# Values of layer 0 weighed in five chunks of 128 head-and-key rows, brought to those rows through DRAM

## The chip, the cores and the metric

The kernel runs on one core of one Trainium2 chip. A core has TensorE (PE; PEld is its weight load), VectorE (DVE), ScalarE (ACT), GpSimd (POOL) and SyncE (SP, which here only issues DMAs and waits), and sixteen DMA engines. The metric is the device time of one execution in microseconds (us), the median of several runs; lower is better.

## The reference, cut to what matters

Two layers, each a cross attention and a mixture of eight experts with a residual path. The change is in the first attention: 32 sequences of 128 tokens (D = 128) look at 77 context rows each, with 8 heads of 64.

```python
q = (x @ Wq).reshape(B, N, 8, 64).transpose(0, 2, 1, 3)        # x: layernorm of the residual, 32 x 128 x 128
k = (context @ Wk).reshape(B, M, 8, 64).transpose(0, 2, 1, 3)  # context: 32 x 77 x 128
v = (context @ Wv).reshape(B, M, 8, 64).transpose(0, 2, 1, 3)
attn = softmax(einsum('bhnd,bhmd->bhnm', q, k) * scale)
out = einsum('bhnm,bhmd->bhnd', attn, v)
x = x + tanh(g_xattn[0]) * (out.transpose(0, 2, 1, 3).reshape(B, N, 512) @ Wo + bo)
# then: expert layer 0, attention of layer 1 (16 heads of 8), expert layer 1
```

## The kernel before

**Products of weights.** Both layer-0 products of two weight matrices are made once: `wqk` (Wq times Wk of a head) and `wvo` (Wv times Wo of a head, 128x128 for each head), each split in a high and a low part (fp32r). So for a sequence b the "value" of a head is directly its contribution to the output: `vo0[key, head, :]`, 77 keys by 8 heads by 128 floats.

**Units and steps.** A unit of layer 0 is one sequence. `attention0_steps` writes out by hand the order of the work: step u holds `score0(u)` (six matmuls into two PSUM banks), `exp0(u)`, `weigh0(u - 2)`, the two halves of the values `v0(u, 0)` and `v0(u, 1)` (four heads each, three matmul passes of 77x512 into the one bank `V_BANK`), `divide0(u)`, `turn0(u - 1)`, `bias0(u)`, and among them pieces of the keys of the next group of four sequences (`k0`), its layernorm (`norm`, `normalize`, `xt`), the routing tasks of groups that are already done (`mturn`, `route`, `pick`, `rank`, `lead`, `scatter`) and one background task a step (context blocks, `("tables", l)`, `("expert", 0, e)`). All five engines walk the same list in its order and each takes the tasks that concern it, so the list is the order of every engine's queue. SP runs ahead in it until something that it waits for isn't done.

**One unit of layer 0.** DVE takes the row maximum and subtracts it (L1243, L1246), ACT takes the exponential (L1122), DVE sums (L1297) and inverts, POOL divides (L1598). PE transposes the eight heads of 77 keys apart into two banks (`turn0`, L830), ACT copies both banks to `prob_t` (L1136; every fourth unit DVE copies the second one, L1305). ACT copies each half of the values from `V_BANK` to `vo0` (L1127), which PE must wait for before the next half. PE then adds up eight products of 77 rows (`weigh0`, L850); each is recorded as two instructions, sixteen in all. DVE adds the result to the residual (L1311).

```python
for head in range(NH0):
    done = pe.matmul(banks[:, O_BANK, 0:D], prob_t[0:NKEY, b % 2, head, :], vo0[:, b % 2, head, :],
                     start=head == 0, stop=head == NH0 - 1)
```

**Layer 1** already works in chunks: 8 heads of 77 keys lie one behind the other, 616 rows, cut into `CHUNKS` = 5 chunks of 128, 128, 128, 128 and 104 rows. `turn1` transposes five chunks (L840) and `weigh1` adds up five products (L866, ten recorded instructions).

**Waits.** `w.wait_ge(name, n)` blocks the engine until a semaphore has reached n; everything behind it on that engine waits too. A DMA adds 16 when it has landed.

Of the kernel before, what the change touches and what calls it, by code (L numbers as in the profile page):

```python
# [17 lines left out]
ALU = mybir.AluOpType  # L18
ACT = mybir.ActivationFunctionType
# [6 lines left out]
P = 128  # L26
# [251 lines left out]
def order():  # L278
# [3 lines left out]
    out += first[1:] + [("wvo", 0), ("wvo", 1), ("ctx", 1), ("gates",)]  # L282
# [24 lines left out]
def flamingo_two_layers(nc, a, out):  # L307
# [49 lines left out]
    y_rows = [nc.dram_tensor(f"y_rows{k}", [(2 * HT + NO_TOKEN) * P, D], F32, kind="Internal").ap() for k in range(2 * HALVES)]  # L357

# [4 lines left out]
    with ExitStack() as stack:  # L363
        def sbuf(name, shape, dt=F32):
            return stack.enter_context(nc.sbuf_tensor(name, shape, dt))
# [71 lines left out]
        prob_t = sbuf("prob_t", [P, 2, UH, SEQ])  # L437
# [63 lines left out]
        vo0 = layer0_only.enter_context(nc.sbuf_tensor("vo0", [NKEY, 2, NH0, D], F32))  # L501
# [101 lines left out]
        def _(sync):  # L603
# [29 lines left out]
            for t in plan:  # L633
# [25 lines left out]
                elif t[0] == "tail":  # L659
# [3 lines left out]
                    sync.dma_start(x_rows[k][bass.ds(r, P), :], empty_rows[e * P:(e + 1) * P, :]).then_inc(sem("tails"), 16)  # L663
                elif t[0] == "fetch":
# [73 lines left out]
        def _(pe):  # L738
# [86 lines left out]
            def turn0(b):  # L825
                w.wait_ge("divided", b + 1)
                for k in (0, 1):
                    w.wait_ge(f"prob_t{k}", b)
                    for i in range(4):
                        done = pe.transpose(banks[0:NKEY, PT_BANK[k], i * SEQ:(i + 1) * SEQ], prob[:, b % 2, 4 * k + i, :], ident[:, :])  # L830
                    done.then_inc(sem("prob_turned"))

            def turn1(u):
                flat = prob1_of(u).rearrange("p h n -> p (h n)")
                w.wait_ge("exp", NSEQ + u + 1)
                w.wait_ge("xb", LAYER_BLOCKS)
                for k, chunks in enumerate(CHUNK_SETS):
                    w.wait_ge(f"prob_t{k}", NSEQ + u)
# [4 lines left out]

            def weigh0(b):
                w.wait_ge("prob_t0", b + 1)
                w.wait_ge("prob_t1", b + 1)
                w.wait_ge("v0", 2 * b + 2)
                w.wait_ge("x_attn", b)
                for head in range(NH0):
                    done = pe.matmul(banks[:, O_BANK, 0:D], prob_t[0:NKEY, b % 2, head, :], vo0[:, b % 2, head, :],  # L850
                                     start=head == 0, stop=head == NH0 - 1)
                done.then_inc(sem("pv"))

            def weigh1(u):
                b, half = u // 2, u % 2
                width = UH * DV1
                w.wait_ge("prob_t0", NSEQ + u + 1)
                w.wait_ge("prob_t1", NSEQ + u + 1)
# [19 lines left out]
            for t in plan:  # L878
# [107 lines left out]
                elif kind == "turn":  # L986
# [3 lines left out]
                    for k in (0, 1):  # L990
                        w.wait_ge(f"prob_t{k}", NSEQ + layer * U1)
# [57 lines left out]
        def _(act):  # L1049
# [12 lines left out]
            for t in plan:  # L1062
# [60 lines left out]
                elif kind == "v0":  # L1123
                    b, h = t[1:]
                    w.wait_ge("v0_mm", 2 * b + h + 1)
                    w.wait_ge("pv", b - 1)
                    act.activation(vo0[:, b % 2, 4 * h:4 * h + 4, :].rearrange("p h d -> p (h d)"), banks[0:NKEY, V_BANK, :],  # L1127
                                   ACT.Copy).then_inc(sem("v0"))
                elif kind == "turn0":
                    b = t[1]  # L1130
                    for k in (0, 1):
                        if k == 0 or b % 4 > 0:
                            w.wait_ge("prob_turned", 2 * b + k + 1)
                            w.wait_ge("pv", b - 1)
                            dst = prob_t[0:NKEY, b % 2, 4 * k:4 * k + 4, :].rearrange("p s n -> p (s n)")
                            act.activation(dst, banks[0:NKEY, PT_BANK[k], :], ACT.Copy).then_inc(sem(f"prob_t{k}"))  # L1136
# [570 lines left out]
```

## Time and profile before

| | |
|---|---|
| three runs of the kernel before | 857.03, 858.85 and 860.1 us, median 858.85 |
| profiled execution | 851.79 us, of it 849.8 us from the first to the last instruction |
| busy: PE, PEld, DVE | 694.9 (82%), 630.4 (74%), 569.2 (67%) us |
| busy: ACT, POOL | 454.3 (53%), 478.6 (56%) us |
| mean granted TensorE clock | 0.95 of full |
| layer-0 attention | first `weigh0` at 45.0 us, last at 259.8 us |

The program is four phases one after the other, with small overlaps: layer-0 attention, its experts, layer-1 attention, its experts. Busy shares are means over all of them; what limits the first phase has to be read within it. A matmul record lasts longer than the distance to the next one, since matmuls are pipelined: how long a group of them holds PE is read from the chain of work, where each piece runs until the next begins.

### The profile page before, as it was taken

Reading aid. Unit: us, or ns where it says so; the run is one execution under the profiler, and the core shown is the slowest. Engines: PE = TensorE matmul, PEld = TensorE weight load, DVE = VectorE, ACT = ScalarE, POOL = GpSimd, SP = SyncE. Lnnn points to the kernel's source line nnn. Section 1 sums busy time; section 2 is a strip of 40 time slices with the busy share of each in tenths; the row PEclk is TensorE's granted clock in tenths of the full one; section 3 lists DMA queues with packets and bytes.
Section 4 is the critical chain, followed back from the end, with each engine's and each line's share of the span. In section 5 each row is a group of like instructions: output and inputs, shape, how many; then the busy total and the mean of one; then the engine's idle time right before and its main releaser. Section 6 shows DMA issues by size and latency. Waiting matters only on the chain.

```text
span 849.8 us, 17654 instructions
## 1 busy us (share of the span) xinstructions
PE 694.9 (82%) x5008; PEld 630.4 (74%) x5008; DVE 569.2 (67%) x2013; ACT 454.3 (53%) x1211; POOL 478.6 (56%) x693
## 2 busy tenths in 40 slices
PE   5899998997997668888879988988788847578688
PEld 4789987887886658777768887777678737567577
DVE  2668877886675555787887877977876725344553
ACT  3467675764555425555656776577476623233333
POOL 4233366664477555685554435667566766655562
PEclk9999999997999879999998999999999989799999
DMA  9334000001102222444633535533433022233445
GB/s 263 113 99 127 1 22 19 25 22 43 33 32 74 64 78 82 120 109 119 168 83 90 115 69 108 118 93 69 123 90 70 25 84 80 85 94 109 133 130 179
DMA packets 89934, 75.74 MB, mean 89 GB/s; under 512 B 28872, under 2 KB 78056, under 8 KB 89776
## 3 DMA queue, kind: packets, MB, share of 16 engines
q1 hardware_dynamic: 72144, 48.96, 23.3%
q0 software_dynamic: 9088, 19.68, 7.2%
q10 hardware_dynamic: 8608, 5.99, 2.5%
q8 instruction: 42, 0.69, 0.4%
q14 instruction: 52, 0.43, 0.2%
HBM read 44.99 MB, written 34.00 MB: 93 GB/s over the span
## 4 chain that ended last, share of the span: by engine, by line
PE 46%; DVE 20%; ACT 13%; issue 9%; another core or an unknown queue 8%; DMA 1%; DVEq 1%; POOL 0%; SPq 0%; POOLq 0%; ACTq 0%
PE banks L1003 8%; PE banks L1022 5%; PE banks L866 5%; PE banks L850 5%; PE banks L742 3%; DVE row_max L1243 3%; PE banks L806 2%; PE banks L744 2%; PE banks L925 2%; PE banks L743 2%; PE banks L830 2%; DVE prob L1246 2%; PE banks L840 2%; DVE hidden L1496 1%
## 5 line engine op out<-in xcount | busy, mean ns | idle before, releaser
L1677 POOL DMA_INDIRECT y_rows<-y_sb,result_at x156 | 152.8, 980 | 114.0 <-DVE result_at L1476 56.5
L1003 PE MATMUL banks<-xb,up 128*128 128x128 f32 x936 | 147.7, 298 | 65.0 <-ACT xb L1186 20.7
L1003 PEld LDWEIGHTS banks<-xb,up 128*128 128x128 f32 x936 | 128.1, 207 | 75.1 <-issue 43.1
L1670 POOL DMA_INDIRECT x_rows<-xm,row x128 | 127.5, 996 | 34.8 <-issue 30.4
L1022 PE MATMUL banks<-down,hidden 128*128 x624 | 104.6, 294 | 15.1 <-DVE y_sb L1513 6.7
L1022 PEld LDWEIGHTS banks<-down,hidden 128*128 128x128 f32 x624 | 89.0, 206 | 20.6 <-issue 20.2
L1632 POOL TENSOR_TENSOR v_flat<-v_raw,row_head 104x64 f32<-104x64 f32 (+1 forms) x128 | 55.9, 462 | 80.6 <-ACT v_raw L1165 80.0
L866 PE MATMUL banks<-v_flat,prob_t 128*128 128x108 f32 (+2 forms) x640 | 85.4, 282 | 6.7 <-ACT prob_t L1149 3.6
L866 PEld LDWEIGHTS banks<-v_flat,prob_t 128*128 128x128 f32 (+1 forms) x640 | 78.8, 195 | 16.0 <-ACT prob_t L1149 8.6
L1203 ACT ACTIVATE gate<-banks,block_bias 128x128 f32<-128x128 f32 x156 | 48.7, 365 | 74.9 <-PE banks L1003 47.8
L1243 DVE TENSOR_REDUCE row_max<-banks 128x8 f32<-128x616 f32 x96 | 75.8, 790 | 16.6 <-PE banks L821 8.9
L1598 POOL TENSOR_TENSOR prob<-prob,inv_sum 128x616 f32<-128x616 f32 x32 | 38.9, 1217 | 72.1 <-DVE inv_sum L1300 72.0
L1207 ACT ACTIVATE hidden<-banks 128x256 f32<-128x256 f32 x78 | 29.9, 384 | 92.3 <-remote 41.2
L1513 DVE COPY y_sb<-banks 128x128 f32<-128x128 f32 x78 | 22.4, 288 | 75.2 <-remote 35.9
L1496 DVE SCALAR_TENSOR_TENSOR hidden<-banks,block_bias,gate 128x128 f32<-128x128 f32 x156 | 47.0, 342 | 36.2 <-ACT gate L1203 29.8
L850 PE MATMUL banks<-vo,prob_t 77*128 77x128 f32 x512 | 64.7, 281 | 0.0
L850 PEld LDWEIGHTS banks<-vo,prob_t 77*128 77x128 f32 x512 | 63.0, 198 | 0.0
L1488 DVE COPY up<-up 128x256 f32 x156 | 56.1, 360 | 9.4 <-issue 3.9
L1149 ACT ACTIVATE prob_t<-banks 128x512 f32<-128x512 f32 (+1 forms) x128 | 48.8, 437 | 24.7 <-PE banks L840 24.6
L1246 DVE TENSOR_TENSOR prob<-banks,row_max 128x616 f32<-128x616 f32 x75 | 60.0, 800 | 2.6
L1165 ACT ACTIVATE v_raw<-banks 128x512 f32<-128x512 f32 x64 | 28.4, 444 | 44.8 <-PE banks L925 43.8
L1186 ACT ACTIVATE xb<-banks 128x128 f32<-128x128 f32 x156 | 43.4, 278 | 7.3 <-PE banks L993 3.3
(216 smaller groups left out, 1653.9 us busy)
## 6 DMA issues: line engine op xcount, KB each, us to landing
x_norm<-x_rows SPq DMA_DIRECT2D x86, 72.0 KB
x_far<-x_rows SPq DMA_DIRECT2D x70, 72.0 KB
gathered<-y_rows ACTq DMA_DIRECT2D x32, 128.0 KB
q_rows<-up_raw SPq DMA_DIRECT2D x8, 512.0 KB
q_even<-q_rows SPq DMA_DIRECT2D x12, 256.0 KB
q_odd<-q_rows SPq DMA_DIRECT2D x12, 256.0 KB
y_rows<-y_sb,result_at POOLq DMA_INDIRECT x156
k_rows<-up_raw SPq DMA_DIRECT2D x32, 77.0 KB
```

The lines of the kernel that those rows point to most:

```text
L850: done = pe.matmul(banks[:, O_BANK, 0:D], prob_t[0:NKEY, b % 2, head, :], vo0[:, b % 2, head, :], start=head == 0, stop=head == NH0 - 1)
L866: done = pe.matmul(banks[:, O_BANK, half * width:half * width + cols], prob_t[0:rows, u % 2, c, :], v1_flat[0:rows, first:first + cols], s ...
L1003: done = pe.matmul(banks[:, UP_BANK[i % 2], part * P:(part + 1) * P], block_w[:, i % WR, part // 2, part % 2 * P:(part % 2 + 1) * P], xb[: ...
L1022: done = pe.matmul(banks[:, Y_BANK[i % 2], 0:D], hidden[:, i % HR, half, :], of_expert(flat[:, (2 * layer + half) * D:], i, D), start=half ...
L1149: act.activation(dst, banks[0:rows, PT_BANK[k], 0:len(chunks) * SEQ], ACT.Copy).then_inc(sem(f"prob_t{k}"))
L1243: dve.tensor_reduce(m_view, s_view, AX.X, ALU.max).then_inc(sem("row_max"))
L1246: dve.tensor_tensor(prob_view.rearrange("p (k s) n -> p k s n", k=2), s_view, m_view.unsqueeze(3).to_broadcast([P, 2, 4, NKEY]), ALU.subtr ...
L1488: dve.tensor_copy(block_w[:, i % WR, 1 - layer, :], src[:, bass.ds(at, HID1)]).then_inc(sem("block_w_dve"))
L1496: dve.scalar_tensor_tensor(hidden[:, i % HR, half, :], banks[:, UP_BANK[i % 2], (2 + half) * P:(3 + half) * P], block_bias[:, k, 2 + half, ...
L1632: pool.tensor_tensor(v1_rows[0:rows, b % 2, half, chunks[0]:chunks[-1] + 1, :, 0:DK1], v1_raw[0:rows, chunks[0]:chunks[-1] + 1, half, :, : ...
L1670: pool.indirect_dma_start(out=x_rows[i // HG][:, :], out_offset=bass.IndirectOffsetOnAxis(ap=row[:, n, c:c + 1], axis=0), in_=xm[:, i % 2, ...
L1677: pool.indirect_dma_start(out=y_rows[k][:, :], out_offset=bass.IndirectOffsetOnAxis(ap=result_at[:, i % (2 * YR):i % (2 * YR) + 1], axis=0 ...
```

## The change

A unit's transposed probabilities and values are laid out as in layer 1: 616 rows of head and key in five chunks. The probabilities need no extra step, since `prob` lies in that order already. The values come out of the matmul with the key on the partition, so they go to DRAM and come back with head and key on it: each half of `vo0` (now one buffer a half) is written to `v_rows` by SP, and two loads fetch 4x128 and 104 rows into `vo_flat`. The values of sequence u + 1 are made in step u, a unit sooner than before, and those of sequence 0 ahead of step 0. ACT copies all of `prob_t` in layer 0; the two semaphores `prob_t0` and `prob_t1` become one. Two more semaphores (`group_sum`, `block_e`) are folded into `rank_step` and `table_step`, with the same waits.

```diff
         if u < NSEQ:
-            step += [("v0", u, 0), ("divide0", u)] + more[1]
+            step += [("v0_load", u)] + [("v0", u + 1, 0)][:u + 1 < NSEQ] + [("divide0", u)] + more[1]
         if 0 <= u - 1 < NSEQ:
             step.append(("turn0", u - 1))
         if u < NSEQ:
-            step += [("v0", u, 1), ("bias0", u)] + more[2]
+            step += [("v0", u + 1, 1)][:u + 1 < NSEQ] + [("bias0", u)] + more[2]
...
-    out += first[1:] + [("wvo", 0), ("wvo", 1), ("ctx", 1), ("gates",)]
+    out += first[1:] + [("wvo", 0), ("wvo", 1), ("ctx", 1), ("v0", 0, 0), ("v0", 0, 1), ("gates",)]
...
+    v_rows = [nc.dram_tensor(f"v_rows{i}", [UNIT_ROWS, D], F32, kind="Internal").ap() for i in (0, 1)]
...
-        prob_t = sbuf("prob_t", [P, 2, UH, SEQ])
+        prob_t = sbuf("prob_t", [P, 2, CHUNKS, SEQ])
...
-        vo0 = layer0_only.enter_context(nc.sbuf_tensor("vo0", [NKEY, 2, NH0, D], F32))
+        vo0 = layer0_only.enter_context(nc.sbuf_tensor("vo0", [NKEY, 2, NH0 // 2, D], F32))
+        vo_flat = layer0_only.enter_context(nc.sbuf_tensor("vo_flat", [P, 2, CHUNKS, D], F32))
...
+                elif t[0] == "v0":
+                    b, h = t[1:]
+                    half_rows = v_rows[b % 2][h * (UNIT_ROWS // 2):(h + 1) * (UNIT_ROWS // 2), :]
+                    w.wait_ge("v0", 2 * b + h + 1)
+                    w.wait_ge(f"v0_in{b % 2}", 32 * (b // 2))
+                    sync.dma_start(half_rows.rearrange("(a n) d -> n a d", n=NKEY), vo0[:, h, :, :]).then_inc(sem("v0_out"), 16)
+                elif t[0] == "v0_load":
+                    b = t[1]
+                    full = CHUNKS - 1
+                    w.wait_ge("v0_out", 32 * (b + 1))
+                    w.wait_ge("pv", b - 1)
+                    sync.dma_start(vo_flat[:, b % 2, 0:full, :], v_rows[b % 2][0:full * P, :].rearrange("(c p) d -> p c d", p=P)).then_inc(sem(f"v0_in{b % 2}"), 16)
+                    sync.dma_start(vo_flat[0:chunk_rows[full], b % 2, full, :], v_rows[b % 2][full * P:, :]).then_inc(sem(f"v0_in{b % 2}"), 16)
...
             def weigh0(b):
-                w.wait_ge("prob_t0", b + 1)
-                w.wait_ge("prob_t1", b + 1)
-                w.wait_ge("v0", 2 * b + 2)
+                w.wait_ge("prob_t", 2 * (b + 1))
+                w.wait_ge(f"v0_in{b % 2}", 32 * (b // 2 + 1))
                 w.wait_ge("x_attn", b)
-                for head in range(NH0):
-                    done = pe.matmul(banks[:, O_BANK, 0:D], prob_t[0:NKEY, b % 2, head, :], vo0[:, b % 2, head, :],
-                                     start=head == 0, stop=head == NH0 - 1)
+                for c, rows in enumerate(chunk_rows):
+                    done = pe.matmul(banks[:, O_BANK, 0:D], prob_t[0:rows, b % 2, c, :], vo_flat[0:rows, b % 2, c, :],
+                                     start=c == 0, stop=c == CHUNKS - 1)
                 done.then_inc(sem("pv"))
...
                 elif kind == "v0":
                     b, h = t[1:]
                     w.wait_ge("v0_mm", 2 * b + h + 1)
-                    w.wait_ge("pv", b - 1)
-                    act.activation(vo0[:, b % 2, 4 * h:4 * h + 4, :].rearrange("p h d -> p (h d)"), banks[0:NKEY, V_BANK, :],
+                    w.wait_ge("v0_out", 32 * b)
+                    act.activation(vo0[:, h, :, :].rearrange("p h d -> p (h d)"), banks[0:NKEY, V_BANK, :],
                                    ACT.Copy).then_inc(sem("v0"))
```

Left out: `turn0` now transposes the five chunks, as `turn1` does, through a helper `turn_chunks`; ACT's `turn0` copies 128x512 and 104x128; DVE's share of it is gone; the semaphore names.

Two places of the order. On TensorE, one step of the dense part before (`wvo_h` passes are `v0`, `wqk_h` passes are `k0`, `ident,prob` is `turn0`, `vo,prob_t` is `weigh0`):

```order
L850 MATMUL banks<-vo,prob_t 128x128 [waits x_attn,prob_t1,prob_t0]
L850 MATMUL banks<-vo,prob_t 128x128 x7
L742 MATMUL banks<-wvo_h,ctx_th 77x512 [waits v0]
L743 MATMUL banks<-wvo_h,ctx_tl 77x512
L744 MATMUL banks<-wvo_l,ctx_th 77x512
L742 MATMUL banks<-ctx_th,wqk_h 128x308 [waits split_lo]
L743 MATMUL banks<-ctx_th,wqk_l 128x308
L744 MATMUL banks<-ctx_tl,wqk_h 128x308
L830 MATMUL banks<-ident,prob 77x128 [waits divided]
L830 MATMUL banks<-ident,prob 77x128 x7
```

and the same place after the change (lines have moved by 14 to 17):

```order
L864 MATMUL banks<-vo_flat,prob_t 128x128 [waits x_attn,v0_in1,prob_t]
L864 MATMUL banks<-vo_flat,prob_t 128x128 x4
L759 MATMUL banks<-wvo_h,ctx_th 77x512 [waits v0]
L760 MATMUL banks<-wvo_h,ctx_tl 77x512
L761 MATMUL banks<-wvo_l,ctx_th 77x512
L759 MATMUL banks<-ctx_th,wqk_h 128x308 [waits split_lo]
L760 MATMUL banks<-ctx_th,wqk_l 128x308
L761 MATMUL banks<-ctx_tl,wqk_h 128x308
L846 MATMUL banks<-ident,prob 128x128 [waits divided]
L846 MATMUL banks<-ident,prob 128x128 x3
L846 MATMUL banks<-ident,prob 104x128
```

Eight products and eight transposes have become five and five; the half of the values between them now belongs to the next sequence.

On SP, the place of `("tables", 0)` and the first two experts after the change. Before, these loads stood alone there, with nothing of a unit between them, and SP issued the eight `up` loads one behind the other:

```order
L673 DMA v_rows<-vo 77x4x128 [waits v0_in1,v0]
L673 DMA v_rows<-vo 77x4x128 [waits v0]
L611 DMA down<-in_L_ffn_Wl_dram 128x8x128 [waits split_mm]
L611 DMA down<-in_L_ffn_Wl_dram 128x8x128
L611 DMA router<-in_L_ffn_Wr_dram 128x8x1
L611 DMA up_raw<-in_L_ffn_bl_dram 8x512
L611 DMA down_bias<-in_L_ffn_bl_dram 128x1024
L611 DMA router_b<-in_L_ffn_br_dram 128x8
L611 DMA select_b<-in_L_ffn_biases_N_dram 128x8
L679 DMA vo_flat<-v_rows 128x4x128 [waits pv,v0_out]
L680 DMA vo_flat<-v_rows 104x128
L673 DMA v_rows<-vo 77x4x128 [waits v0_in0,v0]
```

Four DMAs of a unit stand in SP's queue in every step now: two writes that wait for ACT, two loads that wait for the landing of both writes and for `weigh0` of two units before.

## Rows read from the trace of the kernel before

**Rows 1.** Windows: length, busy us and count of PE, PEld, DVE, ACT, POOL; PE clock, DMA share, GB/s

```profile
54.00:97.00 43.00, 43.00 (x319) 39.74 (x318) 33.49 (x87) 30.53 (x63) 17.28 (x26) 1.00 0.39 110
97.00:206.00 109.00, 97.71 (x708) 88.29 (x707) 86.38 (x304) 66.67 (x143) 66.50 (x89) 0.98 0.08 24
206.00:230.00 24.00, 21.99 (x129) 19.73 (x128) 13.50 (x50) 10.35 (x21) 10.14 (x14) 0.79 0.07 22
```

**Rows 2.** The chain of work, 54 to 262 us, shares by line

```profile
by line: PE banks L850 20.9%; PE banks L806 8.6%; PE banks L742 8.3%; PE banks L830 7.5%; PE banks L744 7.4%; PE banks L743 7.3%; issue 4.4%; ACT vo L1127 4.3%; DVE prob L1246 2.7%; PE banks L953 2.4%; DVE row_max L1243 2.4%; DVE m_stats L1
```

**Rows 3.** The chain in order of time (start, us, what), dense part

```profile
54.03 1.79 PE banks L850 x16
...
62.71 0.87 PE banks L830 x8
...
83.29 1.79 PE banks L850 x16
...
96.68 1.79 PE banks L850 x16
```

**Rows 4.** The chain in order of time, the part with routing

```profile
109.51 1.79 PE banks L850 x16
...
126.65 0.59 ACT vo L1127
...
133.58 0.58 ACT vo L1127
...
179.91 1.79 PE banks L850 x16
```

**Rows 5.** The chain in order of time, 205 to 240 us

```profile
205.75 3.42 PE banks L850 x16
...
218.40 2.31 PE banks L850 x16
...
231.52 1.79 PE banks L850 x16
...
236.89 1.79 PE banks L850 x16
```

**Rows 6.** Line 850: durations in ns (min/median/max), first and last start

```profile
L850 PE MATMUL banks<-vo,prob_t x512: 272/275/422, 45.2 to 259.8; 77*128 77x128 f32 x171
```

**Rows 7.** The chain in layer 1, where five chunks are weighed and transposed

```profile
463.15 1.34 PE banks L866 x10
...
464.92 0.55 PE banks L840 x5
```

**Rows 8.** ACT by shape in layer 1: busy us, mean ns, idle before

```profile
L1149 ACT ACTIVATE prob_t<-banks 104x128 f32<-104x128 f32 x64 | 17.8, 278 | 0.0
```

**Rows 9.** Timeline, the second half of the values of one unit (start, us)

```profile
134.21 0.45 PE L742 MATMUL banks<-wvo_h,ctx_th 128*77 128x512 f32 x1 [0.54 <-ACT vo L1127]
...
135.32 0.60 ACT L1127 ACTIVATE vo<-banks 77x512 f32<-77x512 f32 x1
```

**Rows 10.** Timeline, DMAs with a known end: last store; a write and its reader

```profile
847.67 0.34 ACTq L1232 DMA_DIRECT2D out_dram<-x_res  x1
...
412.40 0.45 SPq L688 DMA_DIRECT2D q_rows<-up_raw  x1
...
415.53 1.28 SPq L710 DMA_DIRECT2D q_even<-q_rows  x3
```

**Rows 11.** DMA view of 2 to 20 us, when the queues are full of 512-byte packets

```profile
DMA packets 10106, 5.20 MB, mean 289 GB/s; under 512 B 1104, under 2 KB 9722, under 8 KB 10106
```

**Rows 12.** Timeline of SP, the issues of the layer-0 tables

```profile
52.25 1.01 SPq L607 DMA_DIRECT2D down<-in_L_ffn_Wl_dram  x2
...
57.02 0.44 SPq L607 DMA_DIRECT2D select_b<-in_L_ffn_biases_N_dram  x1
```

**Rows 13.** Timeline, a pass of the values near the start of the phase

```profile
33.22 0.63 PE L742 MATMUL banks<-wvo_h,ctx_th 128*77 128x512 f32 x1
```

More of the change, by code:

```diff
@@ L823, in score1, with turn_chunks @@
                 done.then_inc(sem("scores"))
[L825 to L836, printed above, removed]
+            def turn_chunks(flat, n):
                 for k, chunks in enumerate(CHUNK_SETS):
-                    w.wait_ge(f"prob_t{k}", NSEQ + u)
+                    w.wait_ge("prob_t", 2 * n + k - 1)
                     for c in chunks:
@@ L856, in weigh1 @@
                 width = UH * DV1
-                w.wait_ge("prob_t0", NSEQ + u + 1)
-                w.wait_ge("prob_t1", NSEQ + u + 1)
+                w.wait_ge("prob_t", 2 * (NSEQ + u + 1))
                 w.wait_ge("v1", 4 * b + 4)
@@ L989, in _ @@
                     w.wait_ge(f"x_in{i % XR}", landed(i % XR, i + 1, XR))
-                    for k in (0, 1):
-                        w.wait_ge(f"prob_t{k}", NSEQ + layer * U1)
+                    w.wait_ge("prob_t", 2 * (NSEQ + layer * U1))
                     w.wait_ge("xb", i - 1)
@@ L1140, in _ @@
                     act.activation(prob1_of(u), prob1_of(u), ACT.Exp, scale=DK1 ** -0.5).then_inc(sem("exp"))
-                elif kind == "turn1":
-                    u = t[1]
+                elif kind in ("turn0", "turn1"):
+                    n = t[1] if kind == "turn0" else NSEQ + t[1]
+                    if kind == "turn1":
+                        w.wait_ge("up", LAYER_BLOCKS)
                     for k, chunks in enumerate(CHUNK_SETS):
                         rows = chunk_rows[chunks[0]]
-                        w.wait_ge("prob_turned", 2 * NSEQ + 2 * u + k + 1)
-                        w.wait_ge("pv", NSEQ + u - 1)
-                        w.wait_ge("up", LAYER_BLOCKS)
-                        dst = prob_t[0:rows, u % 2, chunks[0]:chunks[-1] + 1, :].rearrange("p s n -> p (s n)")
-                        act.activation(dst, banks[0:rows, PT_BANK[k], 0:len(chunks) * SEQ], ACT.Copy).then_inc(sem(f"prob_t{k}"))
+                        w.wait_ge("prob_turned", 2 * n + k + 1)
+                        w.wait_ge("pv", n - 1)
+                        dst = prob_t[0:rows, n % 2, chunks[0]:chunks[-1] + 1, :].rearrange("p s n -> p (s n)")
+                        act.activation(dst, banks[0:rows, PT_BANK[k], 0:len(chunks) * SEQ], ACT.Copy).then_inc(sem("prob_t"))
                 elif kind == "v1":
@@ L1300, in _ @@
                     dve.reciprocal(inv_sum[:, b % 2, 0:UH], row_sum[:, b % 2, :]).then_inc(sem("inv_sum"))
-                elif kind == "turn0" and t[1] % 4 == 0:
-                    b = t[1]
-                    w.wait_ge("prob_turned", 2 * b + 2)
-                    w.wait_ge("pv", b - 1)
-                    dve.tensor_copy(prob_t[0:NKEY, b % 2, 4:8, :].rearrange("p s n -> p (s n)"), banks[0:NKEY, PT_BANK[1], :]).then_inc(sem("prob_t1"))
                 elif kind == "weigh0":
@@ L1395, in _ @@
                     w.wait_ge("counts", i)
-                    dve.tensor_reduce(group_sum[:, :], picked[:, s, :, :].bitcast(F32).rearrange("p j e -> p e j"), AX.X, ALU.add).then_inc(sem("group_sum"))
-                    w.wait_ge("group_sum", i + 1)
+                    dve.tensor_reduce(group_sum[:, :], picked[:, s, :, :].bitcast(F32).rearrange("p j e -> p e j"), AX.X, ALU.add).then_inc(sem("rank_step"))
+                    w.wait_ge("rank_step", 3 * i + 1)
                     k = i // HG
```

33 lines of the change are left out of this document (16 added, 17 removed).

## The prediction

> **What bounds the kernel now.** I first cut the layer-0 attention, the only phase that the change touches, into stretches with the table of windows. From 54 to 97 us TensorE is busy for all of 43.0 us, DVE for 33.5 and ACT for 30.5; from 97 to 206 us, where routing is mixed in, TensorE has 97.7 of 109, DVE 86.4; from 206 to 230 us TensorE has 22.0 of 24 at a granted clock of 0.79 [rows 1]. Then I read the chain of work over 54 to 262 us: `weigh0` (L850) alone holds 20.9% of it and `turn0` (L830) 7.5%, and the six longest lines are all TensorE's [rows 2]. In order of time the chain shows what a piece costs where it counts: `weigh0` 1.79 us for its sixteen records, 0.112 us each, and `turn0` 0.87 us for eight, 0.109 each [rows 3]. Last, the chain of the routed part shows where TensorE isn't what ends last: after the `vo` copy at 126.65 us it goes through ACT and DVE (the routing's small operations, row maximum, subtraction) to ACT's exponential and the `vo` copy at 133.58 us behind it, for which TensorE stands still [rows 4]. A `weigh0` inside such a stretch is free today.
>
> **What is removed.** Six of sixteen records of `weigh0` go: 6 x 0.112 = 0.67 us a unit. Three of eight transposes go: 3 x 0.109 = 0.33 us. The nearest rows for the new shapes are layer 1's, which does the same five chunks: ten records 1.34 us, five transposes 0.55 us [rows 7]. The transposes agree (5 x 0.109 = 0.54); the ten records there are followed by a wait, so their 1.34 holds the tail of the last product, and 1.12 (10 x 0.112) is what I take where the next product follows at once; by 1.34 the saving would be 0.45. So 1.0 us a unit, at least 0.78. The units that profit are those whose pieces lie on the chain:
> - Dense, 54.03 to 96.68 us: seven units [rows 3], 7 x 1.0 = 7.0.
> - Routed, 97 to 206 us: the chain has nine `weigh0` (the first at 109.51, the last at 179.91 [rows 4]) and six `turn0`: 9 x 0.67 + 6 x 0.33 = 8.0.
> - 206 to 230 us: two slowed `weigh0` of 3.42 and 2.31 us [rows 5], of which 6/16 is 2.1, and a `turn0` slowed likewise: 2.7.
> - 230 to 248 us: two more units of 5.37 us (231.52 to 236.89 [rows 5]), 2.0.
> - The end, 248 to 262 us: two `weigh0` and a `turn0`, 1.7, and the last step has no values to make, so that the copy of the last probabilities comes that much sooner: 0.8. Together 2.5.
>
> That would be 22.2 us if nothing took its place.
>
> **What is added: a loop through DRAM.** ACT may overwrite `vo0` with a half of sequence b + 1 only once both halves of b have landed in DRAM (`v0_out`). So there is now a loop: copy of half 1 of b, its write, then ACT's copy of half 0 of b + 1, then TensorE's passes for half 1 (they need the one bank), then its copy. No row shows such a write, so I bound it. Low end: the last store starts its issue at 847.67 and the span ends at 849.8, 2.1 us for 64 KB of 128 packets [rows 10]. A half is 308 packets of 512 bytes; in full queues a packet takes 16 x 18 / 10106 = 0.0285 us of an engine [rows 11], so 180 packets more on 16 engines are 0.3 us: 2.4. High end: `q_rows`, 512 KB, has its issue at 412.40 and its reader's at 415.53, 3.1 us [rows 10]. I take 2.8, as a half in 512-byte pieces from 77 partitions is not tidier than either, and 0.1 for SP's wakeup: 2.9. The rest of the loop is two copies of 0.59 [rows 4], TensorE's three passes from start to copy, 1.1 (134.21 to 135.32 [rows 9]), and 0.05 for handing over: 2.3. A unit can't be shorter than 2.9 + 2.3 = 5.2 us.
> - Five dense units take 5.85 us now ((83.29 - 54.03) / 5), two 6.7 [rows 3]. The five would be 4.85 and stop at 5.2: 0.35 x 5 = 1.8 us not gained.
> - The units of 5.37 would be 4.4 and stop at 5.2 as well: 1.5 not gained.
> - Over the phase a unit is 6.9 us on the mean ((259.8 - 45.2) / 31 [rows 6]); in the routed part 5.2 never binds.
>
> So 22.2 - 3.3 = 18.9.
>
> The Trainium skill ("DMA: Bandwidth & Descriptors", "Why a DMA increments its semaphore by 16 and not by 1") says that a DMA from SP uses the largest number of engines up to 16 that divides the slowest dimension of both sides; for 77 partitions that is 11. It speaks against this write: 28 packets an engine instead of 19, 0.25 us more a landing, some 2.5 us less gained over the ten units that the loop binds. No row here shows how many engines a DMA took.
>
> **Loads.** Load b is issued once `weigh0(b - 2)` is done and the write has landed, and is needed two steps later, some 10 us. Its 616 packets are 616 x 0.0285 / 16 = 1.1 us [rows 11] on top of a landing like the above: hidden. Writes and loads together hold the DMA engines for 2.2 us of a unit; they are idle 92% of the routed part [rows 1].
>
> **Start.** The two halves of sequence 0 now stand ahead of `score0(0)`. TensorE's passes last 0.63 us there [rows 13], the three some 1.3; the second half must wait for the copy of the first (0.6), so scores begin 3.2 us later. TensorE has little slack behind, and ACT's first copy of step 0 waits for the first landing. Cost 3.0. From below it is 2.2, twice the 1.1 us from passes to copy of [rows 9].
>
> **SP's queue.** Its loads no longer run ahead. The layer-0 tables take SP from 52.25 to 57.46, 5.2 us [rows 12], and now stand between the write of one unit and the load and writes of the next: write (6, 1) leaves 5.2 + four issues of 0.45 [rows 10] = 7.0 us after (5, 1), where the loop has 5.2. That is 1.8 us, once; the second tables come in the routed part with its longer units: 0.2. Cost 2.0. The fetches of the first expert blocks now wait behind `v0_load(31)`, but the first is read two products and a transpose group later: nothing, and 1 us if that cover were gone. ACT's `prob_t` copies become 0.59 + 0.28 [rows 8] for two of 0.59, DVE loses eight copies: both leave slack. The folded semaphores wait for the same events: nothing.
>
> **Sum.** 18.9 - 3.0 - 2.0 = 13.9 us off the profiled 851.8: 837.9. That execution lies 7 us below the median of the runs shown, and nothing in the change touches that distance, so 858.85 - 13.9 = 845.
>
> **The rivals.**
> - **The landing is hidden** (chance 0.17). At 2.4 us the loop is 4.7 and binds almost nothing: 22.2 - 0.5, less 3.0 and 2.0, 16.7 off: 842. For it: SP has little else to do.
> - **DVE takes over** (0.15). In the routed part it has 86.4 us of 109 [rows 1]; with 8 us less it would be busy for 86%, in an order that makes it wait for others. If half the gain from 97 to 230 us goes into its waits, 8.5 are left: 850. Against it: its load falls a little, and its stretches are already counted as not gaining.
> - **The loop through DRAM sets every unit, and the kernel is slower** (0.09). It decides from the point where the loop is longer than the mean unit less what start and tables cost: 6.9 - 5/31 = 6.7 us, a landing of 4.4. At 5.0 the loop is 7.3, 31 x 0.4 + 5 = 18 us more: 877. For it: 512-byte packets, loads and expert weights in the same queue ahead of a write. Against: both ends of the bound are far below.
> - **Nothing to be seen** (0.05). TensorE has more gaps, and its clock falls: from 206 to 230 us it was 0.79 after a stretch with little work [rows 1]. Two more such stretches, each with 24 us of a fifth less clock, cost 10 us: 855 to 859. The Trainium skill ("TensorE: Matmul & The Clock Gate", "HAM oscillation") warns that gaps between bursts bring the half clock back; here the gap that I add is about 0.4 us a unit, and before, the 11 us that TensorE was idle in the routed part left it at 0.98.
>
> **How the numbers follow.** The forecast has 0.54. With the two rivals on its side, faster by over 0.3% (2.6 us, about what a measurement of this kernel can tell) has 0.86, no change 0.05, slower 0.09. The range: below, the hidden landing and a cheap start give 841, and up to 5 us more if routed stretches shrink beyond the chain's own pieces: 836. Above, DVE's 850, and 3 us for a landing at the high end and dear tables: 853. What lies outside is the slower rival, no change, and little else.
>
> **What would show it.** Right: `weigh0` ten records in 1.1 to 1.3 us on the chain; dense units of 5.2 us with ACT's first `vo` copy of a step released by a DMA; a later first `score0`; TensorE no longer full from 54 us on. Wrong: `vo` copies that wait over 1 us for a DMA in most units (landing over 3.5 us), a wait of `weigh0` for a load, or a routed part that still takes 109 us.

## The result, and the profile after

The changed kernel took 855.5 us (median of 17 runs, 850.54 to 861.21) where the kernel before took 859.5 (17 runs, 855.85 to 865.36). The ratio is 0.9950, 95% interval 0.9929 to 0.9971: 4 us faster, where 14 were forecast. The direction was right, the size was not, and 855.5 lies outside the range.

The sum was made on an execution of before that took 851.8 us, faster than every one of its 17 timed runs; the profiled execution of the changed kernel took 861.2. The stages must therefore be compared, not the two totals. These are windows of the changed kernel in the order of [rows 1], with one more at the end (length; busy us and count of PE, PEld, DVE, ACT, POOL; granted clock, DMA share, GB/s):

```profile
54.00:97.00 43.00, 38.72 (x251) 34.03 (x252) 32.47 (x80) 27.97 (x64) 17.33 (x26) 0.96 0.60 162
97.00:206.00 109.00, 93.13 (x589) 81.89 (x587) 88.45 (x303) 65.60 (x150) 66.74 (x88) 0.92 0.47 131
206.00:230.00 24.00, 19.02 (x104) 16.78 (x105) 15.22 (x58) 10.89 (x24) 11.71 (x17) 0.79 0.35 101
230.00:262.00 32.00, 27.00 (x160) 24.10 (x160) 19.69 (x66) 15.30 (x35) 22.09 (x30) 0.79 0.41 116
```

TensorE has less to do in the same 109 us (93.1 busy for 97.7), but at a granted clock of 0.92 for 0.98. Where the clock goes is seen in its timeline (start, us, work, in brackets the idle time before it and what ended it):

```profile
133.89 0.71 PE L846 MATMUL banks<-ident,prob 128*128 128x128 f32 x5
136.67 0.45 PE L759 MATMUL banks<-wvo_h,ctx_th 128*77 128x512 f32 x1 [2.07 <-ACT vo L1139]
...
138.60 1.37 PE L823 MATMUL banks<-k_t,xt_h 128*128 128x308 f32 x4
...
141.05 2.34 PE L864 MATMUL banks<-vo_flat,prob_t 128*128 128x128 f32 x10
```

After `turn0` TensorE stands still for 2.07 us, until ACT's copy of the first half of the values; in before this same gap was 0.54 us [rows 9]. From `score0` on what follows costs nearly double: its four records take 1.37 us and `weigh0` 2.34, where they take 0.8 and 1.3 in the same view at full clock. The windows behind two such gaps have a clock of 0.57:

```profile
110.00:114.00 4.00, 4.00 (x20) 3.95 (x19) 2.42 (x8) 2.90 (x8) 3.20 (x4) 0.57 0.54 144
137.00:143.00 6.00, 5.90 (x27) 5.45 (x26) 3.41 (x10) 3.85 (x9) 3.71 (x4) 0.57 0.41 115
```

ACT's copy is late because it stands behind the exponential, and that behind DVE. ACT's timeline in the gap:

```profile
135.42 0.72 ACT L1134 ACTIVATE prob<-prob 128x616 f32<-128x616 f32 x1 [3.13 <-DVE prob L1251]
136.04 0.57 ACT L1139 ACTIVATE vo<-banks 77x512 f32<-77x512 f32 x1
```

Over 54 to 262 us TensorE waits for that copy 17.8 us in 12 places (the view of waits: total, times, longest); below it the same view of the kernel before:

```profile
PE banks L759 <- ACT vo L1139: 17.8, 12, 2.9
```

```profile
PE banks L742 <- ACT vo L1127: 5.5, 6, 1.7
```

The other thing to see is a hold in SP's queue. The chain of work of the changed kernel, from 66 us on:

```profile
66.69 0.40 SPq L611
...
67.79 1.71 SPq L611
...
69.54 1.62 SPq L611
...
73.59 0.32 SPq L673
...
73.97 4.00 DMA v_rows<-vo
...
78.06 0.60 ACT vo L1139
...
81.67 1.93 PE banks L864 x10
```

The tables hold the queue from 66.69 us; the two loads of a unit follow at 72.59 and 73.02, and the two writes of the next unit's values at 73.59 and 73.97. The second one lands only at 78.0, with an expert's weights issued right behind it; ACT's copy waits for the landing, and `weigh0` then runs at a low clock again.

### The profile page after: what moved, and what is told of

It is laid out like the page before. It is cut to its first block, busy times and chain, and to the rows that moved or that the text cites. A ratio compares the mean times of both kernels' runs of the same rounds, so it can differ in the third digit from the quotient of the medians.

```text
span 859.4 us, 17242 instructions
## 1 busy us (share of the span) xinstructions
PE 684.9 (80%) x4720; PEld 618.0 (72%) x4720; DVE 566.5 (66%) x2005; ACT 448.8 (52%) x1219; POOL 480.2 (56%) x693
## 4 chain that ended last, share of the span: by engine, by line
PE 41%; DVE 23%; ACT 12%; issue 10%; another core or an unknown queue 7%; DMA 2%; SPq 1%; DVEq 1%; POOL 1%; ACTq 0%; POOLq 0%
PE banks L1015 10%; PE banks L1034 7%; PE banks L879 4%; DVE row_max L1248 4%; PE banks L864 3%; DVE prob L1251 3%; PE banks L759 2%; PE banks L846 2%; PE banks L823 2%; PE banks L938 2%; PE banks L761 2%; PE banks L760 2%; ACT x_norm L1117 2%; ACT vo L1139 1%
## 5 line engine op out<-in xcount | busy, mean ns | idle before, releaser
L1015 PE MATMUL banks<-xb,up 128*128 128x128 f32 x936 | 150.3, 302 | 66.4 <-ACT xb L1191 25.4
L1015 PEld LDWEIGHTS banks<-xb,up 128*128 128x128 f32 x936 | 130.8, 211 | 76.5 <-issue 41.4
L1034 PE MATMUL banks<-down,hidden 128*128 x624 | 104.9, 295 | 16.6 <-DVE y_sb L1513 10.4
L1154 ACT ACTIVATE prob_t<-banks 128x512 f32<-128x512 f32 x192 | 73.1, 436 | 24.7 <-PE banks L846 22.3
L1488 DVE COPY up<-up 128x256 f32 x156 | 53.6, 344 | 9.1 <-issue 4.2
L846 PE MATMUL banks<-ident,prob 128*128 128x128 f32 (+1 forms) x375 | 56.5, 284 | 0.0
L864 PE MATMUL banks<-vo_flat,prob_t 128*128 128x128 f32 (+1 forms) x320 | 48.1, 305 | 3.3 <-ACT prob_t L1154 3.3
L864 PEld LDWEIGHTS banks<-vo_flat,prob_t 128*128 128x128 f32 (+1 forms) x320 | 46.6, 222 | 3.4 <-ACT prob_t L1154 3.4
```

Source lines behind the costliest of these rows:

```text
L846: done = pe.transpose(banks[0:chunk_rows[c], PT_BANK[k], c % 4 * SEQ:(c % 4 + 1) * SEQ], flat[:, c * P:c * P + chunk_rows[c]], ident[:, :])
L864: done = pe.matmul(banks[:, O_BANK, 0:D], prob_t[0:rows, b % 2, c, :], vo_flat[0:rows, b % 2, c, :], start=c == 0, stop=c == CHUNKS - 1)
L1015: done = pe.matmul(banks[:, UP_BANK[i % 2], part * P:(part + 1) * P], block_w[:, i % WR, part // 2, part % 2 * P:(part % 2 + 1) * P], xb[: ...
L1034: done = pe.matmul(banks[:, Y_BANK[i % 2], 0:D], hidden[:, i % HR, half, :], of_expert(flat[:, (2 * layer + half) * D:], i, D), start=half ...
L1154: act.activation(dst, banks[0:rows, PT_BANK[k], 0:len(chunks) * SEQ], ACT.Copy).then_inc(sem("prob_t"))
L1488: dve.tensor_copy(block_w[:, i % WR, 1 - layer, :], src[:, bass.ds(at, HID1)]).then_inc(sem("block_w_dve"))
```

## The experiments

All kernels were compared with before on their own chip. There before took 792 us instead of 859. The 67 us do not lie in this phase: in a second profile of before `score0(25)` starts at 198.99 us, in the first at 199.13. So ratios are given, and 0.001 is 0.8 us. An interval of a ratio is 0.002 to 0.004 to each side.

What separates the kernels better is their profiles. This table has the start of `score0(n)` in us, read from TensorE's timeline of each, and the start of the last record of the last `weigh0`. Each row is one execution:

```
kernel       ratio    s(0)   s(1)   s(4)   s(8)  s(11)  s(25)  s(31) weigh0(31)
before       1       30.45  36.93  58.37  81.87 100.99 199.13 246.63 259.8
before_look  0.9998  30.44  36.81  58.24  81.73 100.84 198.99 248.59 261.8
after        0.9950  33.72  39.95  60.79  85.79 103.14 202.30 248.52 261.4
again        0.9948  33.74  39.98  61.62  86.98 103.84 201.12 246.66 259.4
pad          1.0018  33.84  40.07  61.35  86.56 105.65 207.15 250.90 264.1
nodma        0.9899  33.84  40.07  60.37  81.34  98.22 197.27 243.60 256.4
keep         0.9898  34.27  40.51  60.81  86.91 104.14 197.10 238.66 254.9
deep         0.9884  33.72  39.96  60.25  81.23  98.12 194.96 238.44 252.0
tables       0.9903  33.55  39.80  60.11  81.16  98.19 195.50 240.83 253.8
start        0.9964  29.79  39.47  60.99  86.74 103.38 201.76 247.13 260.7
best         0.9798  30.25  38.83  59.12  80.09  96.96 189.92 233.87 249.9
before_keep  1.0037  30.14  36.76  58.22  81.71 100.82 206.34 254.06 267.2
ideal        0.9834  30.14  36.52  56.80  77.78  94.66 187.65 229.28 246.3
best2        0.9872  34.15  40.38  60.67  81.64  98.52 191.51 232.98 249.0
keep_gaps    0.9911  34.20  40.43  60.73  86.16 103.20 196.42 238.01 250.7
best3        0.9830  30.16  39.10  59.41  80.39  97.25 190.26 231.65 245.2
best3_four   0.9808  29.68  38.30  59.30  80.28  97.14 190.41 236.75 249.5
ideal3       0.9815  30.17  36.54  56.85  77.85  94.71 187.75 229.22 241.8
```

The theories. **Clock**: the shorter work leaves longer gaps in the steps that DVE ends, in them TensorE's clock falls to half, and that gives the gain back. **Detour**: the way through DRAM and SP's queue costs it. **Order**: DVE ends last in the routed part, so that the gain turns into waits.

**again**, the changed kernel once more.

> The changed kernel once more, beside which the other kernels of this group stand. Both theories: 855 us, 0.995 of before. What it tells is how far the profiled execution of 861.2 us is from a usual one: if the half clock after the gaps of the routed part (109 to 114 us, 137 to 143 us) is there again, it belongs to the kernel; if the clock is at 1.00 there, that execution was an exception and the clock can't be what took the gain.

0.9948 (0.9922 to 0.9975), as in the first comparison; the clock in 97 to 206 us is 0.94, in 230 to 262 us 0.82, and in the two windows of 110 to 114 and 137 to 143 us 0.73 and 0.72. The half clock belongs to the kernel.

**before_look**, the kernel before once more.

> The kernel before once more, so that the profiled execution on which the prediction's sum was made can be set beside another one. If 851.8 us was an ordinary execution, its clock was 1.00 in 97 to 202 us and 230 to 262 us and will be so again, and score0(31) starts at 246.6 us; if it was a lucky one, the clock is lower in one of them and score0(31) comes 2 to 5 us later.

The same kernel to `score0(25)` within 0.2 us, then 2.0 us later at `score0(31)`: from 206 to 230 us its clock was 0.70, in the first profile 0.79 [rows 1]. Its row:

```profile
206.00:230.00 24.00, 23.26 (x124) 20.67 (x122) 12.39 (x48) 8.47 (x18) 9.94 (x13) 0.70 0.06 19
```

The first profile was 2 us lucky in this phase. Differences of 2 us behind 206 us are therefore not read as effects below.

**pad**, TensorE's records put back.

```diff
 def weigh0(b):
+    for c in (0, 1, 2):
+        pe.matmul(banks[:, O_BANK, 2 * D:3 * D], prob_t[:, b % 2, c, :], vo_flat[:, b % 2, c, :], start=True, stop=True)
...
 # turn_chunks, ahead of chunk 4, layer 0
+    for i in (1, 2, 3):
+        pe.transpose(banks[0:chunk_rows[4], PT_BANK[1], i * SEQ:(i + 1) * SEQ], flat[:, 4 * P:4 * P + chunk_rows[4]], ident[:, :])
```

> The changed kernel with TensorE's records put back: six records of three idle products ahead of each layer-0 weigh0 and three idle transposes ahead of the fifth one in turn0. The values still go through DRAM and are made a unit sooner; the sum is unchanged. Clock theory (the shorter work makes gaps in which the clock falls): only start and tables remain as costs, 5 us, so 859.5 + 5 = 864 us, with the clock of 97 to 206 us back at 0.98. Detour theory (the way through DRAM and SP's queue eat the gain of 22 us down to 4): all 18 us of cost show, 877 us. If DVE's order takes the gain, the clock stays as in the changed kernel and the time is near 860.

1.0018 (0.9991 to 1.0045): 1 us more than before, not 5 and not 18. The order theory had the time (860) but not the clock, which rose. The 1 us is a net figure: `pad` lies 8.2 us behind `before_look` at `score0(25)` and 2.3 at `score0(31)`; from 206 to 230 us its clock is 0.93, and that of before 0.79 and 0.70. Against `again`, six records and three transposes less a unit were worth 5.5 us, though they are 32 us of work. And `pad` had the higher clock, 0.97 from 97 to 206 us and 0.95 from 230 to 262 (again: 0.94 and 0.82). From `score0(25)` to `score0(31)` the kernel with more work is the faster one, 43.8 us against 45.5.

```profile
97.00:206.00 109.00, 101.76 (x722) 92.51 (x721) 84.73 (x291) 66.34 (x151) 64.21 (x85) 0.97 0.46 129
...
230.00:262.00 32.00, 28.18 (x205) 25.68 (x203) 22.90 (x77) 15.89 (x36) 22.72 (x31) 0.95 0.47 132
```

**nodma**, no way through DRAM.

```diff
 # weigh0
-    w.wait_ge(f"v0_in{b % 2}", 32 * (b // 2 + 1))
+    w.wait_ge("v0", 2 * b + 2)
...
-    vo_flat[0:rows, b % 2, c, :]
+    wvo_h[0:rows, c, :].bitcast(F32)
 # ACT, copy of the values
-    w.wait_ge("v0_out", 32 * b)
 # SP: v0 and v0_load issue nothing
```

> The changed kernel without the way through DRAM: the values are made and copied in the same places, but not written and not loaded; weigh0 takes its five right sides from a weight in SBUF instead and waits for the values' copy (the output then lacks the values). Clock theory: about what the changed kernel takes, less the tables' 2 us and the loop, 850 to 853 us, with low clocks in the routed part. Detour theory: the gain of 22 us less 3 for the start comes out, 841 us.

0.9899 (0.9861 to 0.9937), 4 us less than `again`: inside the clock theory's 850 to 853 us (0.989 to 0.992), far from the detour theory's 841. Its clock from 97 to 206 us is 0.90, so the low clock needs no DMA. The table tells where the 4 us come from: all of it, 5.6 us, is there at `score0(11)`. From 11 to 25 this kernel takes 99.05 us, more than `again` (97.28) and than before (98.15): without any DMA the routed part gains nothing. The detour theory fails for that part.

**keep**, work for TensorE in the gaps.

```diff
 # TensorE, ahead of the wait for the bank, second half of the values
+    if h == 1 and b in (12, 16, 20, 24, 28):
+        for _ in range(8):
+            pe.matmul(banks[96:P, V_BANK, 0:D], ident[:, 96:P], ident[:, :], start=True, stop=True, tile_position=(0, 96))
     w.wait_ge("v0", 2 * b + h)
 # and eight more ahead of weigh0(30) and of weigh0(31)
```

> The changed kernel with idle products that keep TensorE at work where it waits: eight 128x128 products (1.8 us at full clock) into the unused last 32 partitions of the bank, ahead of the second half of the values of sequences 12, 16, 20, 24 and 28, and eight ahead of each of the last two weigh0. Clock theory: the clock stays at 1.00 from 97 to 206 us and the time falls by 4 to 8 us, to 847 to 851. Detour theory: 855, no change. Order theory (DVE ends last): 855 to 857.

0.9898 (0.9867 to 0.9929), 4 us less than the changed kernel for work that computes nothing, as the clock theory had it; the clock from 97 to 206 us is 0.98 (1.00 had been expected), from 206 to 230 us 1.00. From 11 to 25 it takes 92.96 us, 4.3 less than `again`. That is no chance of two executions: the six five-chunk kernels here without such products (after, again, nodma, deep, tables, start) take 96.8 to 99.2 us from 11 to 25, the seven with eight of them in each gap 93.0 to 93.2; from 25 to 31 it is 43.5 to 46.3 for 41.4 to 43.9. The timeline that bears out the clock theory is that of `keep_gaps` (below), which has the same five places, at the gap shown above:

```profile
132.65 0.71 PE L846 MATMUL banks<-ident,prob 128*128 128x128 f32 x5
133.29 1.93 PE L912 MATMUL banks<-ident 128*32 128x128 f32 x16
135.64 0.46 PE L759 MATMUL banks<-wvo_h,ctx_th 128*77 128x512 f32 x1 [0.42 <-ACT vo L1142]
...
137.11 0.81 PE L823 MATMUL banks<-k_t,xt_h 128*128 128x308 f32 x4
...
138.46 1.27 PE L864 MATMUL banks<-vo_flat,prob_t 128*128 128x128 f32 x10
```

The wait ends at the same event, ACT's copy; only the idle time is filled. `score0`'s four records take 0.81 us again, `weigh0` 1.27.

**before_keep**, the same products in the kernel before (sequences 11, 15, ..., since its order makes values a unit later).

> The kernel before with the same idle products (eight of 128x128 into the unused last 32 partitions of the values' bank, ahead of the second half of the values of sequences 11, 15, 19, 23 and 27, where the changed kernel has its long gaps). Clock theory: before has gaps of 0.5 us there and a clock of 0.98, so that the products can only delay: 1.000 to 1.005 of before. If idle products help any kernel of this kind, 0.995.

1.0037 (1.0015 to 1.0059), slower, as forecast: from 11 to 25 it takes 105.5 us for 98.15. Idle products are no help in themselves; they help where the change has opened a gap.

**deep**, four half buffers.

```diff
-    vo0 = ... [NKEY, 2, NH0 // 2, D]
+    vo0 = ... [NKEY, 4, NH0 // 2, D]
 # ACT, copy of the values
-    w.wait_ge("v0_out", 32 * b)
+    w.wait_ge("v0_out", 32 * (b - 1))
 # ... SP and ACT take vo0[:, b % 2 * 2 + h, :, :] for vo0[:, h, :, :]
```

> The changed kernel with four half buffers for vo0 instead of two: ACT's copy for sequence b waits for the writes of b - 2, not of b - 1, so that no copy waits for a landing. Detour theory (the loop through DRAM costs as much as it takes): up to 3.3 us of the loop and the 3 us wait behind the tables come back, 4 to 5 us less than the changed kernel, 0.990 of before. Clock theory: only the wait behind the tables matters (ACT's 2.9 us at 76 us, once), and half of it moves on to weigh0's wait for its load: 1 to 2 us less, 0.993.

0.9884 (0.9846 to 0.9922). At `score0(8)` it is 5.75 us ahead of `again`. From `score0(6)` (71.23 and 72.61 us) to `score0(8)` it takes 10.0 us against 14.4: the stall behind the tables costs 4.4. The rest was there by `score0(3)`, where the clock of `again` was 0.68 from 52 to 57 us, after two waits of 1.5 us, and here 1.00 after the same waits. From 8 to 11 both take 16.9 us, and so does `nodma`: where the tables are not in the way, the loop through DRAM binds nothing.

**tables**, the layer-0 tables in four parts in four steps: two halves of `down`, `router`, the rest.

> The changed kernel with the layer-0 tables issued in four parts in four steps instead of eight DMAs in one step; they are the same DMAs. Theory that the tables' hold on SP's queue costs 3 to 4 us: the write of sequence 7's second half starts 3 us sooner, ACT doesn't wait 2.9 us at 76 us, score0(8) is back at 83.5 us from 87.0, and the time is 0.991 of before. Theory that the gain went only through the clock: 0.995, since what comes sooner there makes longer gaps in the routed part.

0.9903 (0.9867 to 0.9939), with the first theory; `score0(8)` is 5.8 us sooner than in `again`, as with `deep`, where 3.5 had been expected. Each of the two removes the same stall, which cost 4.4 us where I had put 2.0.

**start**, the values of sequence 0 behind `score0(0)`.

> The changed kernel with the two halves of the values of sequence 0 behind score0(0) instead of ahead of it. Theory that the start costs 3 us that stay: score0(0) at 30.5 us, and 3 us less than the changed kernel, 0.991 of before. Rival: the chain of step 0 then waits for the landing (the copy for sequence 1 waits for both writes of 0), and nothing is left of it at score0(2): 0.995.

0.9964 (0.9939 to 0.9990): the rival was right. `score0(0)` comes 3.9 us sooner, `score0(1)` only 0.5: the copy for sequence 1 now waits for the landing of the writes of sequence 0. The chain of this kernel shows the landing by itself, and gives the time of a write with nothing in the queue but the other half's write, 1.6 us ahead: 2.28 us from its issue on SP.

```profile
34.92 2.28 DMA v_rows<-vo
37.23 0.05 issue
37.28 0.60 ACT vo L1139
```

**best**, the last four edits together, and **best2**, the same without the edit at the start.

> All four together: idle products ahead of the late values copies and the last two weigh0, four half buffers, tables in four parts, values of sequence 0 behind the first scores. If the costs are apart from each other: 4 (products) + 3 (start) + 3.5 (tables with the buffers) less than the changed kernel's 0.995, which is 0.982 of before. If what is won ahead of 97 us only lengthens the waits for DVE in the routed part: 0.987.

> The best kernel so far with the values of sequence 0 back ahead of score0(0): idle products, four half buffers and tables in four parts stay. If putting them behind the first scores was worth nothing by itself (0.9964 against 0.9948), this one is equal or better, 0.979; if the start's 1 us is real once nothing else is in the way, 0.982.

0.9798 (0.9762 to 0.9834) and 0.9872 (0.9840 to 0.9905); the second is outside both of its forecasts. At `score0(31)` the gains add up: 5.8 us with `tables` alone, 8.0 with `keep` alone, 13.7 with both in `best2`. So what is won ahead of 97 us does not turn into waits. With four buffers the edit at the start is worth 1.5 us at `score0(1)`; of the 6 us between the ratios the rest has no place in the profiles, since `best2` is even ahead at `score0(31)`.

**ideal**, five chunks alone: order of before, no way through DRAM, idle products.

> Five chunks alone: the order of the kernel before, no way through DRAM (weigh0 takes its right sides from a weight in SBUF, so the output lacks the values), and the idle products in the gaps. It is what the shorter work is worth with neither start nor tables nor clock against it. By the prediction's sum 22 us less, 0.974 of before on a fast chip; if the waits for DVE keep a third of it, 15 us, 0.981.

0.9834 (0.9797 to 0.9871), near the second forecast. It leads `best2` at `score0(31)` by 4 us, but needs 17.0 us from there to the last `weigh0`, where before needs 13.2. The chain of `best` shows why: the idle products that I had put ahead of the last two `weigh0` are on it, at half clock (L864 is their line there, L869 `weigh0`'s).

```profile
245.47 3.41 PE banks L864 x16
248.88 1.31 PE banks L869 x10
```

Four more runs leave those last products out.

> The changed kernel with the idle products in the five gaps alone, without the eight products ahead of each of the last two weigh0, which the profile of the four-part kernel shows on the chain (3.4 us ahead of the last weigh0). Clock theory: the gaps' products bring all of the gain, the last ones cost some 3 us, so 0.986 of before against 0.990 with both. If the last ones held a clock that the end needs, 0.992.

> All four edits (idle products in five gaps, four half buffers, tables in four parts, values of sequence 0 behind the first scores) without the products ahead of the last two weigh0. 0.980 was measured with them; if they cost 3 us, 0.976, with the last weigh0 at 247 us instead of 249.9.

> The kernel before this one in the list with four idle products in each gap instead of eight (0.9 us instead of 1.8). If the clock needs only some work in the gap: 1.00 there, the same time, 0.976. If the second half of the gap is enough to let it fall: low stretches after some of the five gaps and 2 to 4 us more, 0.980.

> Five chunks alone once more (no way through DRAM, the output lacks the values; order of the kernel before; idle products in the five gaps) without the products ahead of the last two weigh0. It sizes the gross term: the prediction has 22.2 us at the end of the last weigh0. If the last products cost 3 us, weigh0(31) is 18.5 us sooner than in the second profile of before (261.8), ratio 0.978; if the end is DVE's anyway, 15.5 as with them.

`keep_gaps` 0.9911 (0.9872 to 0.9951), `best3` 0.9830 (0.9796 to 0.9864), `best3_four` 0.9808 (0.9772 to 0.9844), `ideal3` 0.9815 (0.9779 to 0.9851). Of the forecasts only `best3_four`'s 0.980 was met. The last `weigh0` comes 4.2 to 4.7 us sooner than with the products, but the whole time does not move within its interval; `keep_gaps` is nearer to the forecast in which the end needs them (0.992) than to the other (0.986). Why isn't settled: in the chain of `best3` the end of the phase is handed to DVE and POOL, and its clock from 230 to 262 us is 0.73. Half the products are enough from 11 to 25 (93.3 us against 93.0), and in these two executions not behind 206 us, where the clock is 0.82 with four and 1.00 with eight (`best`, with eight, had 0.97, and 43.9 us from 25 to 31 for 41.4 in `best3`). With four, in `best3_four`:

```profile
206.00:230.00 24.00, 21.76 (x127) 18.80 (x125) 15.42 (x51) 11.63 (x25) 13.29 (x18) 0.82 0.38 105
```

and with eight, in `best3`:

```profile
206.00:230.00 24.00, 21.52 (x154) 18.37 (x153) 17.58 (x60) 12.64 (x28) 16.91 (x22) 1.00 0.49 134
```

`best`, `best3` and `best3_four` beat both kernels, by 1.7 to 2.0% against before, and `best2` by 1.3%; the intervals of the first three overlap, so none is the best of them.

## Why the prediction was wrong

At `score0(31)` the kernels form a ladder from the second profile of before (248.59 us): `ideal3` -19.4; `best2` +3.8 on it (start, and the way through DRAM with nothing in its way); `keep_gaps` +5.0 (tables ahead of the write); `again` +8.6 (no work in the gaps). It ends at -1.9, and weigh0(31) at -2.4. The steps are differences between single executions. Against them, term by term:

- **Saving, 22.2 us.** Measured with `ideal3`: 20.0 us at the last `weigh0`, 18.0 against the first profile. The size for one piece was right: on the chain `weigh0` takes 1.11 us for ten records, `turn0` 0.55 for five. Dense units, `score0(3)` to `score0(10)`, gave 4.9 for 7.0, and routed ones, 11 to 25, 5.1 for some 8.0, as the pieces that become shorter make room for others on the chain (below); 206 us onward gave more than counted, because before itself runs at half clock there (0.70 from 206 to 230 us, 1.00 in `ideal3`). Nearly right in sum, and in part because these errors cancel.
- **Loop through DRAM, 3.3 us.** Wrong: nothing. `deep`, `again` and `nodma` have the same units where no table is in the queue, some of 4.8 and 5.0 us, below the 5.2 of the sum, and a landing with the queue free takes 2.28 us where I took 2.8. The prediction's eleven engines for such a write fit the trace: the 64 writes of `start` update their semaphore 768 times, twelve each, once at the issue and eleven times at the landing.
- **Start, 3.0 us.** Right: 3.3 at `score0(0)` and 3.2 at `score0(1)`.
- **SP's queue, 2.0 us.** The place was right, the size wrong: 4.4 us (5.0 in the ladder). I had the issues nearly (7.0 us between writes, 7.6 in the chain), but took a landing of 2.9; with two loads and the other half ahead of it and an expert's weights behind it, it was 4.0, and the low clock after the wait made `weigh0` 1.93 us instead of 1.11.
- **The clock, nothing.** This is the step that failed. I held it against the clock that "the gap that I add is about 0.4 us a unit", an average, and that 11 idle us had left it at 0.98. The gaps are not spread out. In the timelines of the routed part one gap in each group of four sequences grew: four of them from 0.53 to 0.57 us in before to 2.07 to 2.14, a fifth, at 229 us, from 1.60 to 2.93. That is 0.39 us a unit on the mean, so the average was right, but it falls in one piece. It cost 8.0 us by `keep_gaps` against `again`, 4.1 from 11 to 25 and 4.0 from 25 to 31 (the other 0.6 of the ladder's step lies ahead of the first filled gap). The Trainium skill ("TensorE: Matmul & The Clock Gate", "HAM oscillation") has the mechanism, idle gaps between bursts of matmuls that bring the half clock back, and the trace agrees: four records of `score0` 1.37 us behind the gap, 0.81 with it filled. I had it as a rival with 0.05, at 855 to 859; measured were 855.5. Its mechanism was right, its place in part: it priced 10 us from two more stretches like 206 to 230 us, where half of the loss lies ahead of 206 us, behind gaps of 2 us. Of the prediction's signs of being wrong, a routed part that takes as long as before was met: 97.3 and 99.2 us from 11 to 25, for 98.2.
- **The base.** Differences off a lucky execution: 2.0 us more of half clock in the usual one, all behind 206 us. It moved no term by more than that.

22.2 - 3.3 - 3.0 - 2.0 was 13.9. With measured terms, all at `score0(31)`, it is 19.4 - 3.8 - 5.0 - 8.6 = 2.0. That this is the 1.9 us of the table proves nothing, since the terms are made as differences along it; what they tell is where the 13.9 went, and 8.6 of it is the term that I had at nothing. The whole time gives 4.1 us (2.0 to 6.2). The rival in which DVE takes over (850) has a share of it: DVE makes the gap. But filled with idle work the same order is 8 us faster at `score0(31)`, so waiting alone was not the price.

Why the dense saving is 4.9 instead of 7.0 can be read from the chain. Over 54 to 97 us it is TensorE's throughout in before. In `deep`, where no copy waits for DRAM, it leaves TensorE at 65 us and goes mostly through ACT's exponential and DVE's maximum, subtraction and sum, as it did before only in the routed part:

```profile
67.68 0.69 DVE row_max L1248
68.40 0.81 DVE prob L1251
69.23 0.72 ACT prob L1134
69.98 0.81 DVE row_sum L1302
```

Shown by runs are the clock's share up to the end of the phase, the tables' stall and that the loop costs nothing. Open is how much of it reaches the whole time. Filling the gaps gives 8.7 us at the last `weigh0` (`keep_gaps` against `again`) but only 2.9 in the ratios, 0.9911 for 0.9948, whose intervals overlap; for `keep` it is 4.0. The gains of 16.6 and 20.0 us at the last `weigh0` of `best3` and `ideal3` are 13.5 and 14.7 us in the whole time. So of the 8.6 us at `score0(31)` about half is shown in the whole time.

## What to carry to other kernels

When work is taken from an engine whose clock depends on its being busy, do not average the idle time that this makes: find the steps that another engine ends, add the saving to the gap there, and price what follows at half clock. If such a gap opens, either move real work into it or try idle products there and nowhere else; where the gap was 0.5 us they cost 3 us. And when a DMA that someone waits for is put into a queue, list what is issued ahead of it and right behind it; tables issued in one go cost more (5.0 us) than all of the rest of the detour (3.8).

## What the runs showed of the hardware

- Behind a wait of 2.07 us the granted clock was 0.57 in 137 to 143 us, most of it at half clock, though TensorE had been busy before it. The same wait doesn't always do it: the gap at 162 to 166 us left the clock at 1.00 in that execution (busy 1.86 of 4 us ahead, then 5.94 of 6), and in `again` brought it to 0.72 (1.94 of 4 ahead). Both windows behind it, of the changed kernel and of `again`, are below. Before shows it behind its own long wait of 4.39 us, which ends at 204.62: `weigh0` 3.42 us at 205.75 [rows 5].
- A write of 154 KB in 512-byte packets landed 2.28 us after its issue with the queue free, and 4.00 us behind the tables. Its neighbours in the queue go with this, as the semaphore's updates tell for the second half's write in six traces (`again`, `pad`, `deep`, `start`, `best`, `best3`). With nothing issued behind it, and ahead of it only the other half, at least 1.5 us before, 38 writes landed in 2.26 to 2.61 us. With 256 KB of weights 0.3 us behind in the same place, 11 of 18 took 2.3 us and the others up to 4.10. With loads less than 1.6 us ahead and no weights behind, 8 took 2.7 to 3.9; with both, 10 took 3.2 to 4.3. What is issued later can delay a write, but mostly did not without loads ahead.
- The issue of a DMA on SP took 0.3 to 0.6 us for most between 63 and 75 us, but 1.71 for `router` and 1.62 for `up_raw`.

```profile
166.00:172.00 6.00, 5.94 (x40) 5.16 (x41) 4.77 (x14) 5.01 (x13) 3.72 (x4) 1.00 0.38 107
```

```profile
166.00:172.00 6.00, 6.00 (x34) 5.73 (x34) 4.29 (x12) 4.05 (x10) 3.46 (x5) 0.72 0.28 81
```
